# A fused attention kernel: first scores among the last value units, and ten heads of each group turned by the DMA queue

## The reference, cut to what matters

```
x = x + einsum('bct,bcd->bdt', x, weights[subjects])
q, k, v = x@Wq.T (32 heads), x@Wk.T, x@Wv.T (8 heads of 128)
q, k = rope(rmsnorm(q)), rope(rmsnorm(k))
k_all = concat(k_cache[block_table], k);  v_all = concat(v_cache[block_table], v)
scores = q @ k_all.T * SCALE, old keys beyond cache_seqlens masked
out = x + softmax(scores) @ v_all @ Wo.T
```

## Time and profile before

| | us |
|---|---|
| median of 3 runs | 1056.09 (1053.84 to 1056.35) |
| the profiled execution | 1053.23 |
| its span (first to last instruction) | 1051.4 |
| TensorE busy, of the span | 1002.2 (95%) |
| VectorE / ScalarE / GpSimd busy | 775.6 / 708.5 / 519.7 |
| granted TensorE clock | 0.998 of full speed |
| first scores start | 354.93 |
| the 16 DMA engines, SyncE's queue / GpSimd's queue | 59.8% / 18.7% of the span |

### The profile page before, as it was taken

The page is one execution under the profiler, slowest core; times in us unless marked ns, Lnnn a source line. Parts: engine busy times, 40 slices in busy tenths (PEclk is TensorE's granted clock), DMA queues, the critical chain, the costliest instruction groups (busy, mean ns, idle before and its releaser), DMA issues.

```text
span 1051.4 us, 25156 instructions
## 1 busy us (share of the span) xinstructions
PE 1002.2 (95%) x8585; PEld 806.7 (77%) x8585; DVE 775.6 (74%) x1641; ACT 708.5 (67%) x1959; POOL 519.7 (49%) x642
## 2 busy tenths in 40 slices
PE   4899999999889899999999999999999999999998
PEld 2578888887678688779868968977977886896893
DVE  7789999999997788648737846855864873784680
ACT  5898999988765788647737836745754773683670
POOL 6445666567881356526525534633542652563440
PEclk9999999999999999999999999999999999999999
DMA  6789999989989899749957974983984995697440
GB/s 203 251 280 342 323 386 362 392 282 400 366 283 353 330 347 297 243 133 315 306 165 226 344 224 154 326 274 107 344 262 128 306 311 168 217 349 228 146 157 11
DMA packets 200432, 279.72 MB, mean 266 GB/s; under 512 B 26481, under 2 KB 158065, under 8 KB 197745
## 3 DMA queue, kind: packets, MB, share of 16 engines
q1 hardware_dynamic: 181616, 210.86, 59.8%
q0 software_dynamic: 18688, 67.25, 18.7%
HBM read 231.77 MB, written 46.27 MB: 264 GB/s over the span
## 4 chain that ended last, share of the span: by engine, by line
PE 60%; DVE 13%; DMA 10%; ACT 6%; issue 5%; POOL 3%; SPq 3%; ACTq 0%; DVEq 0%; POOLq 0%
PE ps_o L1320 16%; PE ps_proj L1320 13%; PE ps_o L1445 10%; PE ps_t L1420 6%; DMA vs<-v_pages,v_row 6%; PE ps_s L1409 5%; PE ps_s L1413 5%; PE ps_rt L1375 2%; DMA w_nat<-in_L_cond_Wq 2%; DVE rot L1149 2%; DVE c_stage L1177 2%; DVE probs L1256 2%; POOL probs L807 1%; PE ps_o L1459 1%; SPq L594 1%
## 5 line engine op out<-in xcount | busy, mean ns | idle before, releaser
L807 POOL TENSOR_SCALAR probs<-probs,recip 128x544 f32<-128x544 f32 x256 | 184.1, 719 | 329.6 <-DVE recip L1264 324.2
L1256 DVE CUSTOM_DVE_ANT_0 probs<-ps_s,mask,row_scale 128x544 f32<-128x544 f32 x256 | 200.0, 781 | 163.5 <-PE ps_s L1413 158.1
L944 ACT ACTIVATE probs<-probs,neg_max 128x544 f32<-128x544 f32 x256 | 191.6, 748 | 141.4 <-DVE neg_max L1256 119.3
L1445 PE MATMUL ps_o<-pt_hi,vs 128*128 128x128 f16 x2048 | 213.0, 219 | 4.3 <-DMA vs<-v_pages,v_row 4.2
L951 ACT ACTIVATE pt_hi<-ps_t 128x512 f16<-128x512 f32 x256 | 149.4, 584 | 76.3 <-PE ps_t L1420 74.8
L1445 PE MATMUL ps_o<-pt_lo,vs 128*128 128x128 f16 x1024 | 184.6, 219 | 0.0
L761 POOL TENSOR_TENSOR roped<-rot 128x256 f32<-128x256 f32 x160 | 143.8, 920 | 82.1 <-DVE rot L1141 72.5
L1268 DVE SCALAR_TENSOR_TENSOR pt_lo<-ps_t,pt_hi 128x512 f16<-128x512 f32 x256 | 174.3, 681 | 5.1 <-ACT pt_hi L951 2.2
L1445 PEld LDWEIGHTS ps_o<-pt_hi,vs 128*128 128x128 f16 x2048 | 167.8, 98 | 10.2 <-DMA vs<-v_pages,v_row 6.1
L1320 PE MATMUL ps_proj<-wt_hi,x0t_hi 128*128 128x512 f32 x384 | 159.0, 414 | 8.0 <-DVE x0t_lo L1037 7.0
L793 POOL DMA_INDIRECT vs<-v_pages,v_row x128 | 130.8, 1022 | 56.5 <-PE ps_proj L1320 33.9
(11 more groups left out here) (145 smaller groups left out, 1608.3 us busy)
## 6 DMA issues: line engine op xcount, KB each, us to landing
kt<-k_pages_t SPq DMA_DIRECT2D x512, 128.0 KB
c_nat<-in_L_cond_k_cache SPq DMA_DIRECT2D x32, 512.0 KB, 6.0
q_t<-stage SPq DMA_DIRECT2D x64, 256.0 KB, 6.7
c_nat<-in_L_cond_v_cache SPq DMA_DIRECT2D x32, 512.0 KB, 6.8
qt<-q_t SPq DMA_DIRECT2D x32, 512.0 KB
w_nat<-in_L_cond_Wq SPq DMA_DIRECT2D x8, 1024.0 KB, 7.3
k_pages_t<-c_stage SPq DMA_DIRECT2D x16, 512.0 KB, 5.6
c_nat<-in_L_cond_Wo SPq DMA_DIRECT2D x16, 512.0 KB, 7.5
```

Source lines behind the costliest of these rows:

```text
L807: pool.tensor_scalar(probs_of(i), probs_of(i), col(recip, i), 1.0, ALU.mult, ALU.mult).then_inc(p_norm, 1)
L944: act.activation(pr, pr, ACT.Exp, bias=col(neg_max, i), scale=-1.0, accum_out=col(row_sum, i)).then_inc(a_exp, 1)
L1256: dve.tensor_tensor_reduce(out=probs_of(i), in0=ps_s[:, score_cols(i):score_cols(i) + KEYS], in1=mask[(i // HK) % 2][:, mask_at(i):mask_at ...
L1445: ins = pe.matmul(ps_o[n % 2][:, jl * P:(jl + 1) * P], v[:, part, :], p[i % NPT][:, c, :], start=jl == 0 and c == 0 and k == 0, stop=False ...
```

## The change

Two parts, with a new layout of memory that they need.

**Scores of the first heads.** `ps_proj` moves to the last banks of PSUM, so that `ps_s` lies over the banks of `ps_l0` and `ps_tr`, which are free before the last units. The scores of heads 0, 1 and 2 follow units 93, 94 and 95, and so do their masked maximum, exponential and reciprocal on the other engines. 12 heads of `wo` are split early and 20 late (16 in steps 1 to 31, four in steps 32 to 35); its later loads are spread over the first entries. The four gathers of entry 1's values stand between the first `norm`s.

**Heads 2 to 11 of a group.** From the third group on, those whose i % 32 is 2 to 11 (in the second group 8 to 11, in the first none: 4 + 6 x 10 = 64 heads) are not turned by TensorE. ScalarE and VectorE form both halves of the old keys' 512 columns row by row in SBUF, two steps ahead, with normalizer and scale in one factor `split_by`; SyncE's queue turns the 128x1024 fp16 tile into `pt` with one DMA transpose of 256 KB. GpSimd's `norm` of such a head covers only its 32 new columns. The key pages for a later entry are issued four per step (i % 8 = 5, 6, 7, 0) between those transposes, in the place of sixteen at once.

```
+    DMA_FIRST, DMA_LAST, STAGED = 2, 11, 3
+    def by_dma(i):
+        g, r = divmod(i, GSTEPS)
+        return 0 < i < NP2 and g >= 1 and (DMA_FIRST if g > 1 else 8) <= r <= DMA_LAST
+    def split_rows(i, part):
+        return wo[:, HQ + dma_no(i) % STAGED, part, :]
-    WO_LOADS = {84: 0, 85: 1, 87: 2, 89: 3, 92: 4}
-    WO_EARLY, WO_EARLY_AT = 16, 87
+    WO_LOADS = {84: 0, 86: 1, 88: 2, 91: 3}
+    WO_WITH_KEYS = {1: (5,), 2: (6,), 3: (7,)}
+    WO_EARLY, WO_EARLY_AT, LATE_PAIRS = 12, 87, 32
+    SCORES_AT = NU - 3
-    ps_proj = [psum(f"ps_proj{i}", [P, CH]) for i in range(NPJ)]
     ps_l0 = [psum(f"ps_l0{i}", [P, CH]) for i in range(2)]
     ps_tr = psum("ps_tr", [P, CH])
     ps_rt = [psum(f"ps_rt{i}", [P, CH]) for i in range(2)]
+    ps_proj = [psum(f"ps_proj{i}", [P, CH]) for i in range(NPJ)]
...
 SyncE
+            def turn_rows(i):
+                sp.wait_ge(v_plo, dma_no(i + 1))
+                sp.wait_ge(t_pv, i - NPT + 1)
+                sp.dma_start_transpose(pt[i % NPT][:], wo[:, HQ + dma_no(i) % STAGED].rearrange("p s f -> p (s f)")
+                                       ).then_inc(d_pt[i % NPT], 16)
+            PAGES_IN = {5: 0, 6: 4, 7: 8, 0: 12}
+            for i in range(NP2):
+                if by_dma(i + 2):
+                    turn_rows(i + 2)
+                b, r = divmod(i, HK)
+                n = b + 2 if r >= 5 else b + 1
+                if 2 <= n < B and r in PAGES_IN:
+                    if r == 5:
+                        load_queries(n)
+                    load_pages(n, PAGES_IN[r], NPP // len(PAGES_IN))
+                if r == 2 and 1 <= b < B - 1:
+                    load_new_v(b + 1)
...
 GpSimd
+                part = new_keys(i) if by_dma(i) else probs_of(i)
+                pool.tensor_scalar(part, part, col(recip, i), 1.0, ALU.mult, ALU.mult).then_inc(p_norm, 1)
...
 ScalarE
+            def rows_hi(i):
+                act.wait_ge(v_split, dma_no(i + 1))
+                before = [h for h in range(i) if by_dma(h)][-STAGED:]
+                if len(before) == STAGED:
+                    landed(act, before[0])
+                act.activation(split_rows(i, 0), old_keys(i), ACT.Copy, scale=col(split_by, i)).then_inc(a_phi, 1)
...
+                if by_dma(i + 2):
+                    rows_hi(i + 2)
-                if i < NP2:
+                if i < NP2 and not by_dma(i):
                     t_hi(i)
...
 VectorE
+            def rows_lo(i):
+                dve.wait_ge(a_phi, dma_no(i + 1))
+                dve.scalar_tensor_tensor(split_rows(i, 1), old_keys(i), col(split_by, i), split_rows(i, 0),
+                                         ALU.mult, ALU.subtract).then_inc(v_plo, 1)
...
 TensorE
+                if u == SCORES_AT:
+                    pe.wait_ge(v_scale, 3)
+                    pe.wait_ge(v_wsum, HK)
+                if u >= SCORES_AT:
+                    scores(u - SCORES_AT)
...
-                pe.wait_ge(v_tlo, i + 1)
+                if by_dma(i):
+                    landed(pe, i)
+                else:
+                    pe.wait_ge(v_tlo, pe_no(i + 1))
...
-                if i < NP2:
+                if i < NP2 and not by_dma(i):
                     transpose_p(i)
```

More of the change, by code:

```diff
@@ L261, in build @@
     t_pv, t_pvn = sem("t_pv"), sem("t_pvn")
+    d_pt = [sem(f"d_pt{i}") for i in range(NPT)]
+    v_split, a_phi, v_plo = sem("v_split"), sem("a_phi"), sem("v_plo")
     v_rec, p_norm, a_mask = sem("v_rec"), sem("p_norm"), sem("a_mask")
@@ L824, in _ @@
                     wo_low(late_head(i - 1))
+                if i == 0:
+                    pool.wait_ge(t_proj, NU)
+                if i < NCH:
+                    load_v(1, i)
                 b, rest = divmod(i - 2, HK)
@@ L1476, in project_out @@
                     ins.then_inc(t_y, 1)
-            for i in range(AHEAD):
-                scores(i)
+            pe.wait_ge(p_zero, 5)
+            weight_sum(0)
+            l0(0)
+            turn_x(0)
+            l0(1)
+            for u in range(NU):
+                c, g = units[u]
+                if c == 0:
+                    pe.wait_ge(v_xlo, g + 1)
+                if g == 0:
+                    pe.wait_ge(v_wlo, HPC * (c + 1))
+                if u >= NPJ:
+                    pe.wait_ge(v_proj, u - NPJ + 1)
+                tok = slice(g * P, (g + 1) * P)
+                pairs = []
+                for k in range(KC):
+                    hi, lo = x0t_hi[:, k, tok], x0t_lo[:, k, tok]
+                    wh, wl = wt_hi[c % 2][:, k, :], wt_lo[c % 2][:, k, :]
+                    pairs += [(hi, wh), (hi, wl), (lo, wh)]
+                products(ps_proj[u % NPJ][:], pairs).then_inc(t_proj, 1)
+                if u == SCORES_AT:
+                    pe.wait_ge(v_scale, 3)
+                    pe.wait_ge(v_wsum, HK)
+                if u >= SCORES_AT:
+                    scores(u - SCORES_AT)
+                if c == 0 and g + 1 < NG:
+                    turn_x(g + 1)
+                if c == 0 and g + 2 < NG:
+                    l0(g + 2)
+                if LAG <= u < NN + LAG:
+                    un = u - LAG
+                    pe.wait_ge(p_sum, un + 1)
+                    if un == 1:
+                        pe.wait_ge(v_wsum, 2)
+                    if un >= 2:
+                        pe.wait_ge(v_rtlo, un - 1)
+                    for j in range(HPC):
+                        last = pe.transpose(turned_head(un, j), roped[un % NRP][:, j, :], ident[:])
+                    last.then_inc(t_rt, 1)
+                if sum_in(u) is not None:
+                    weight_sum(sum_in(u))
+                if u - TOP_STEP in TOPS:
+                    which = TOPS[u - TOP_STEP][0]
+                    cols = TOP_COLS[which]
+                    pe.wait_ge(v_tops, cols.stop)
+                    pe.transpose(ps_l0[0][0:cols.stop - cols.start, P * which:P * (which + 1)], tops[:, cols], ident[:]).then_inc(t_top, 1)
+                if u - 2 * TOP_STEP in TOPS:
+                    which = TOPS[u - 2 * TOP_STEP][0]
+                    cols = TOP_COLS[which]
+                    n = cols.stop - cols.start
+                    pe.wait_ge(v_diag2, which + 1)
+                    pe.matmul(top_ps(which), ones_p[0:n, :], top_diag[0:n, cols], start=True, stop=True).then_inc(t_bcast, 1)
```

326 lines of the change are left out of this document (154 added, 172 removed).

## The result

The changed kernel takes 1041.82 us, the median of 4 runs (1039.44 to 1046.1), against 1054.96 us of 4 runs before (1051.99 to 1056.35): ratio 0.9883, 95% interval 0.9857 to 0.991. That is 13 us less, where 28 were forecast (1027). The profiled execution is the one of 1046.1 us, with a span of 1044.3 and a mean granted clock of 0.993 of full speed; the other three have 0.997 or 0.998.

A forecast was written before the change was run, and what follows sets the result against it. TensorE, busy 95% of the span, was taken as the bound. 1053.2 - 28.2 (transposes) - 2.5 (end of phase 1) + 2.8 (light steps) = 1025.3; half of 2.9 us added gave 1027 us, range 1014 to about 1052.

The forecast's parts named there:

- Transposes removed: TensorE in phase 2: four transposes per head gone, 0.44 us for each of 64 heads, 28.2 us, all counted.
- the splits at the start of the range: Light steps where a group's queue-turned heads begin: 2 x 0.7 us more split work, held by three heads' lead, counted zero.
- without that cover: ScalarE and VectorE: slower SBUF splits, 8 and 4 us, would cost 12 us if not hidden beside heavy steps.
- The light steps: Steps 10 and 11 of a group: 0.9 us shorter, so the gather wait grows 0.4 us in seven groups, +2.8 us.
- End of phase 1: First transposes start near 356.9 us, 2.3 earlier; -2.5 us taken, between 0 and -4.
- a further gain in the first group: First group of phase 2: spread `wo` loads could take some of its 4 us; zero counted, -3 in the range.
- in or beside heavy steps: Steps 32 to 35: the four more `wo` heads split there lie in or beside heavy steps, counted zero.
- X: Time one queue transpose holds the 16 DMA engines: 1.0 to 1.5 us, free below 1.63, counted zero; likeliest to fail.
- My own formula: DMA engines: transposes longer than 1.63 us exceed the room, costing 64 us for each us above it.
- Landing: From a transpose's issue to its data in `pt`: 4 to 6 us, so no wait of `weigh`; at 9.7, 8 us.
- rival 3: Queue transposes: eight 128x128 blocks run in series, each a whole small transfer; some 2500 us; chance 0.04.

The follow-up runs named there:

- e15: The changed kernel with only heads 2 and 3 of a group turned by the queue (12 heads): 1058.62 us, ratio to before 1.0043.
- e2: The changed kernel with only heads 4 to 11 of a group turned by the queue (52 heads): 1033.25 us, ratio to before 0.9803.
- e14: The changed kernel with heads 3 to 11 by the queue (58 heads) and the last four `wo` splits one step later: 1039.1 us, ratio to before 0.9863.
- e10: The changed kernel with VectorE's and ScalarE's row splits of heads 2 and 3 cut to 32 of 512 columns: 1042.84 us, ratio to before 0.9887.
- e7: The changed kernel with heads 4 to 11 by the queue and the last four `wo` splits one step later: 1032.63 us, ratio to before 0.9801.
- e6: The changed kernel with only heads 4, 5, 7 to 9 and 11 by the queue (39 heads): 1035.67 us, ratio to before 0.9826.
- e4: The changed kernel with the DMA transposes left out, weighing what stands in `pt`: 1041.63 us, ratio to before 0.9895.
- e3: The changed kernel with plain DMA copies of the same bytes in place of the 64 DMA transposes: 1043.63 us, ratio to before 0.9883.

## Why the prediction was wrong

The direction, the cut per head and the end of phase 1 were right; the size was half, and 1041.82 lies 15 us above the forecast, inside its range.

- **Transposes removed, -28.2 us.** Right for each head: 0.44 us between scores. In a group TensorE's busy time falls from 84.4 to 80.4 us, 4.0 for ten heads and not 4.4.
- **The step that failed: the splits at the start of the range.** I wrote "both kinds fall into one step ... the three heads of lead hold that. I count zero", and of the transposes "all are bound by TensorE, so I count all of it". The lead is of `pt`; it doesn't help values with no lead. The maximum frees the bank for the next scores, and `ot_lo` is wanted by the projection at once. Both stand in the queues of VectorE and ScalarE behind the added splits. The runs showed in its place a stretch of 4.05 us for 2.60 in each of six groups. That is 1.45 x 6 = 8.7 us added; and head 2's transposes, which stood inside it, gave nothing by going, 0.44 x 6 = 2.6 us: 11.3 together. The waits say the same, 10.4 - 3.1 = 7.3 us more for `ot_lo` and 6.5 - 2.4 = 4.1 for `neg_max`; the prediction named 12 us "without that cover", by another working. e15 shows the stretch of 4.05 with these two heads alone, e2 shows it gone, e14 shows 0.65 us of it with one head's row splits, and e10 shows 0.80 go with their length.
- **How close e2 and e7 come is in part luck.** With heads 4 to 11 the forecast's own terms give 1027 + 12 x 0.44 = 1032.3; e2 measured 1033.25 and e7 1032.63. But both have the wait behind the residual add, which the sum lacks, and not the 2.8 us of the light steps, which it has.
- **Not in the sum: the wait behind the residual add.** 2.5 + 1.2 = 3.7 us. I costed the removed transposes as free time, and they had covered that add; in e6, where they are back, these waits are gone.
- **The light steps, +2.8 us.** Wrong sign in this trace: waits for `vs` and `kt` fell from 5.7 to 2.2 us. They are 3.7 in e2, 6.6 in e7, 3.4 in e4 and 7.8 in e3, so one trace doesn't settle the term, and why they differ is open.
- **End of phase 1, -2.5 us.** The first transposes came within 0.2 us of the forecast, which is partly luck, as they start anywhere from 354.24 to 358.35 in the traces of the variants. The range named a further gain in the first group; instead 1.7 of 2.4 us were lost there, 1.2 of them at the four `wo` splits that I had placed "in or beside heavy steps": they stand right ahead of the first projection, where the stretch grew from 3.37 to 4.59 us (3.97 with them one step later).
- **X.** 1.8 us, above the 1.0 to 1.5 assumed and above the 1.63 that were to be free, and yet without cost to the median that can be told: e3 at 0.7 us and e4 at none take the same time. My own formula would have made it (1.8 - 1.63) x 64 = 11 us, about 1038 us, close to the measured time by a cause that e4 rules out. The room was larger than my windows gave; the group is 83 us long and not 81, which is part of it at most. The step I called the likeliest to fail was not the one.
- **Landing.** 4.0 us in the median, at the low end of the 4 to 6. The tail to 11.8 us was not foreseen: one late head cost about 6 us in the profiled run.

Together, as an estimate with the waits of the one trace: 1027 + 11.4 + 3.7 + 1.7 - 0.9 (the first group's part in the 7.3 us of `ot_lo`, 1.9 against 1.0) - (2.8 + 3.5) for the light steps = 1036.6; the 0.4 us of busy time a group, 2.6, makes 1039.2. The rest up to 1041.8 is not accounted for; the four runs spread over 6.7 us.

The Trainium skill (VectorE: DVE Perf Modes, "The three transpose paths") has 1309 ns for one 128x128 block. Here eight blocks land after 2.8 us at the least, 0.35 us each, so they don't follow each other at that price, and rival 3 falls. The Trainium skill (DMA: Bandwidth & Descriptors, "Latency and other measured facts") has 261 GB/s for one kernel's transposes. Here, by the queue's share, these took 0.262 MB in 1.8 us, 145 GB/s, beside other traffic; for this kernel the measured figure decides.

What stays open: the 0.65 us of the stretch that e10 leaves, what makes a landing late in some executions, and why the executions of one variant differ by 10 us and more, without the transposes too (e4: 1038.43 to 1051.55 us).
